# Six graph-attention layers on one core: layer 1's transposed input in another PSUM bank, and another order for the last group's layers

## What is computed

```python
# layer 0: 8 heads of width 32, biases, output projection
q, k, v = x @ Wq + bq, x @ Wk + bk, x @ Wv + bv
x = norm(x + concat_heads(softmax(mask(q k^T / sqrt(32))) v) @ Wo + bo)
# layer 1: one head of width 256, no projection biases
x = norm(x + softmax(mask((x Wq)(x Wk)^T / 16)) (x Wv) Wo + bo)
# layers 2 to 5: q and k of width 128 with biases, values are x itself, then Wc
x = norm(x + softmax(mask(q k^T / sqrt(128))) x Wc^T)
```

## Time and profile before

| | us |
|---|---|
| median of 3 runs | 2370.72 |
| lowest and highest run | 2369.71, 2372.63 |
| profiled execution, its own time | 2373.87 |
| span of its instructions | 2372.1 |
| TensorE busy in it | 2259.9 (95%) |
| DVE, ACT, POOL busy | 1783.3 (75%), 1620.0 (68%), 1794.9 (76%) |
| mean granted TensorE clock | 0.99 |

### The profile page before, as it was taken

One profiled execution on the slowest core, in us unless ns is written; L12 is line 12 of the kernel. 1 busy time (PEld: TensorE's weight loads), 2 busy tenths in 40 slices (PEclk: granted clock), 3 DMA queues, 4 the chain that ended last, 5 costly groups with the idle time before them and its releaser, 6 DMA issues.

```text
span 2372.1 us, 59576 instructions
## 1 busy us (share of the span) xinstructions
PE 2259.9 (95%) x20624; PEld 2136.2 (90%) x20624; DVE 1783.3 (75%) x7734; ACT 1620.0 (68%) x5515; POOL 1794.9 (76%) x2399
## 2 busy tenths in 40 slices
PE   6899999999999999999999999999999999999985
PEld 5799999999999999999999999999999999999974
DVE  4777777777877877877877877877777777777864
ACT  5667767767767767767767767766766766767742
POOL 3368878878878878878878878878878878878751
PEclk9999999999999999999999999999999999999998
DMA  4000000100110000010010000000010010000000
GB/s 154 20 23 24 30 28 24 30 28 25 29 28 25 29 28 26 28 28 26 28 28 27 27 28 28 26 28 28 26 28 28 26 28 28 26 29 17 15 10 14
DMA packets 38747, 68.78 MB, mean 29 GB/s; under 512 B 4400, under 2 KB 12848, under 8 KB 37936
## 3 DMA queue, kind: packets, MB, share of 16 engines
q1 hardware_dynamic: 38448, 64.97, 9.0%
HBM read 48.18 MB, written 16.78 MB: 27 GB/s over the span
## 4 chain that ended last, share of the span: by engine, by line
PE 80%; DVE 9%; ACT 7%; issue 2%; POOL 1%; DMA 0%; POOLq 0%; SPq 0%; DVEq 0%
PE value_bank L450 17%; PE qk_bank L442 16%; PE context_bank L595 9%; PE unit_bank L450 7%; PE unit_bank L442 7%; PE qk_bank L549 7%; PE score_bank L579 5%; ACT probs L676 5%; PE unit_bank L506 4%; PE unit_bank L518 3%; DVE scores L820 2%; PE score_bank L576 2%; PE score_bank L586 2%; DVE xT_lo L854 2%; DVE scores L860 1%
## 5 line engine op out<-in xcount | busy, mean ns | idle before, releaser
L1046 POOL TENSOR_TENSOR x<-y,rows 128x512 f32<-128x512 f32 x305 | 392.0, 1285 | 188.9 <-DVE y L913 188.9
L698 ACT CAST xT_hi<-qk_bank 128x512 fp32r<-128x512 f32 x320 | 187.7, 587 | 399.8 <-PE qk_bank L549 399.6
L676 ACT ACTIVATE probs<-scores,negmax 128x128 f32<-128x128 f32 x1024 | 399.1, 393 | 88.6 <-DVE negmax L820 88.6
L913 DVE TENSOR_SCALAR y<-y,mv,rstd 128x256 f32<-128x256 f32 x730 | 304.2, 459 | 191.6 <-POOL rstd L1030 191.3
L442 PE MATMUL qk_bank<-xT_hi,w_lo 128*128 128x256 f32 x1280 | 411.5, 321 | 21.6 <-DVE xT_lo L854 21.3
L1054 POOL TENSOR_TENSOR x<-x,rows 128x512 f32<-128x512 f32 x305 | 393.8, 1291 | 19.2
L450 PE MATMUL value_bank<-w_lo,xT_hi 128*128 128x256 f32 x1280 | 394.4, 308 | 0.0
L442 PE MATMUL qk_bank<-xT_lo,w_hi 128*128 128x256 f32 x1280 | 363.5, 284 | 0.0
L442 PE MATMUL qk_bank<-xT_hi,w_hi 128*128 128x256 f32 x1280 | 362.1, 283 | 0.0
L450 PE MATMUL value_bank<-w_hi,xT_lo 128*128 128x256 f32 x1280 | 361.8, 283 | 0.0
L450 PE MATMUL value_bank<-w_hi,xT_hi 128*128 128x256 f32 x1280 | 361.0, 282 | 0.0
(11 more groups left out here) (93 smaller groups left out, 6503.3 us busy)
## 6 DMA issues: line engine op xcount, KB each, us to landing
x0T<-xT_in SPq DMA_DIRECT2D x64, 256.0 KB, 3.0
x<-x_in SPq DMA_DIRECT2D x64, 256.0 KB, 3.0
out<-x_out SPq DMA_DIRECT2D x64, 256.0 KB, 2.3
adj<-adj_in SPq DMA_DIRECT2D x64, 128.0 KB, 2.2
late_weights<-w_in SPq DMA_DIRECT2D x2, 1024.0 KB, 7.1
rows<-rows_in SPq DMA_DIRECT2D x1, 1792.0 KB, 11.7
probs0T<-w_in SPq DMA_DIRECT2D x4, 256.0 KB, 4.2
x<-w_in SPq DMA_DIRECT2D x1, 1024.0 KB, 13.2
```

What stands on the lines that cost most here:

```text
L676: e = act.activation(probs0[:, j, g, quad], scores0[:, j, g, quad], ACT.Exp, scale=-1.0, bias=negmax0[:, j, g, quad:quad + 1], accum_out=t ...
L913: m = dve.tensor_scalar(y[:, r, g], y[:, r, g], mv[:, r, g, 0:1], rstd[:, r, g:g + 1], ALU.subtract, ALU.mult)
L1046: pool.tensor_tensor(result(norm), y[:, NORM_AT[norm] % YS], row_of_each(f"gamma{layer}"), ALU.mult).then_inc(zg_ready, 1)
```

## The change

1. For layer 1 of groups 1 to 63, the transposed input goes to `unit_bank[0]`, a bank of layer 0, instead of `qk_bank`. TensorE's transposition waits for the next group's first row maximum (which has read that bank) instead of for ACT's move out of `qk_bank`; that second wait moves to `project_qk`. The next group's transposed probabilities of unit 0 wait for the `xT` copy.
2. The plain copy `xT` moves out of `split_hi` to a place behind the softmax of the item before (`move_xT`), and `split_lo` no longer waits for it.
3. The layers of group 63 stand three slots apart: 315, 318, 321, 324, 327. The items behind slot 315 are 316 5/60, 317 4/61, 318 2/63, 319 3/62, 320 5/61, 321 3/63, 322 4/62, 324 4/63, 325 5/62, 327 5/63. Scores are made early from slot 318, the late half of the values is dropped there, and slot 315's norm takes the DVE-only form.
4. The loops of TensorE, ACT and DVE stop after slot 320. The last seven items p to e (3/62, 5/61, 3/63, 4/62, 4/63, 5/62, 5/63) follow in orders written out by hand. SP and POOL keep their loops.

```diff
-MOVED = {LAST_FIRST + 11: LAST_FIRST + 13}
+MOVED = {LAST_FIRST + 4: LAST_FIRST + 3, LAST_FIRST + 3: LAST_FIRST + 4, LAST_FIRST + 6: LAST_FIRST + 5,
+         LAST_FIRST + 8: LAST_FIRST + 6, LAST_FIRST + 12: LAST_FIRST + 9, LAST_FIRST + 11: LAST_FIRST + 10,
+         LAST_FIRST + 16: LAST_FIRST + 12}
+LAST_ITEMS = [LAST_FIRST + n for n in (4, 5, 6, 7, 9, 10, 12)]
+LOOP_SLOTS = range(FIRST, LAST_ITEMS[2])
...
-    return not item(i + 1) or i > LAST_FIRST + STEP
+    return not item(i + 1) or i >= LAST_FIRST + 3
...
+    return norm[1] < STEP * (LAYERS - 3) or norm[1] >= LAST_FIRST
...
-    return i % PERIOD == STEP
+    return i % PERIOD == STEP and i < LAST_FIRST
...
+        def xT_bank(i):
+            return unit_bank[0] if item(i)[0] == 1 and NTH[i] > 0 else qk_bank
...  # transpose_probs0
+                if j == 0 and group > 1:
+                    pe.wait_ge(xT_ready, group)
...  # transpose_x
-                if NTH[i] > 0:
+                psum = xT_bank(i)
+                if psum is not qk_bank:
+                    pe.wait_ge(negmax0_ready, after_unit(min(group + 1, GROUPS - 1), 0))
+                elif NTH[i] > 0:
                     pe.wait_ge(qk_ready, NTH[i])
...  # project_qk
+                if xT_bank(i) is not qk_bank:
+                    pe.wait_ge(qk_ready, NTH[i])
+                elif layer == 1:
+                    pe.wait_ge(xT_ready, group + 1)
...  # TensorE, after the loop
+            p, q, a, b, c, d, e = LAST_ITEMS
+            context(p); project_qk(a); transpose_probs(q); project_v(a, 0); score(a)
+            context(q); project_v(a, 1); transpose_x(b); transpose_probs(a); context(a)
+            project_qk(b); project_v(b, 0); score(b); project_v(b, 1); transpose_x(c)
+            transpose_probs(b); project_qk(c); context(b); project_v(c, 0); score(c)
+            project_v(c, 1); transpose_probs(c); context(c); transpose_x(d); project_qk(d)
+            project_v(d, 0); transpose_x(e); score(d); project_v(d, 1); project_qk(e)
+            transpose_probs(d); project_v(e, 0); score(e); context(d); project_v(e, 1)
+            transpose_probs(e); context(e)
...  # ACT
-                if layer == 1:
-                    act.copy(flat3(xT[:, :]), qk_bank[:, :]).then_inc(xT_ready, 1)
+            def move_xT(i):
+                act.wait_ge(xT_lo_ready, after(i))
+                act.copy(flat3(xT[:, :]), xT_bank(i)[:, :]).then_inc(xT_ready, 1)
...
                 if item(i - 1):
                     softmax(i - 1)
+                if item(i) and item(i)[0] == 1:
+                    move_xT(i)
...  # ACT, after the loop
+            split_hi(a); move_v(q); softmax(q); move_qk(a); move_probsT(q); softmax(a); move_v(a)
+            split_hi(b); move_probsT(a); move_qk(b); softmax(b); split_hi(c); move_probsT(b)
+            move_v(b); move_qk(c); softmax(c); move_v(c); move_probsT(c); split_hi(d); move_qk(d)
+            split_hi(e); move_v(d); softmax(d); move_qk(e); move_probsT(d); softmax(e); move_v(e)
+            move_probsT(e)
...  # DVE: split_lo, and normalise_alone cut in two
-                if layer == 1:
-                    dve.wait_ge(xT_ready, group + 1)
-                else:
-                    dve.wait_ge(xT_hi_ready, after(i))
+                dve.wait_ge(xT_hi_ready, after(i))
+            def normalise_alone(norm):
+                finish(norm, centre(norm))
...  # DVE, after the loop
+            row_max(q); split_lo(a); add_residual(p); statistics(p); reciprocal_total(q)
+            normalise_alone(p); row_max(a); add_residual(q); statistics(q); reciprocal_total(a)
+            split_lo(b); add_residual(a); statistics(a); centred = centre(a); row_max(b)
+            finish(a, centred); split_lo(c); normalise_alone(q); reciprocal_total(b)
+            add_residual(b); row_max(c); statistics(b); reciprocal_total(c); normalise_alone(b)
+            add_residual(c); statistics(c); split_lo(d); normalise_alone(c); split_lo(e)
+            row_max(d); reciprocal_total(d); add_residual(d); row_max(e); statistics(d)
+            reciprocal_total(e); normalise_alone(d); add_residual(e); statistics(e)
+            normalise_alone(e)
```

More of the change, by code:

```diff
@@ L61 @@
 LAST_FIRST = PERIOD * (GROUPS - 1)
-MOVED = {LAST_FIRST + 11: LAST_FIRST + 13}
+MOVED = {LAST_FIRST + 4: LAST_FIRST + 3, LAST_FIRST + 3: LAST_FIRST + 4, LAST_FIRST + 6: LAST_FIRST + 5,
+         LAST_FIRST + 8: LAST_FIRST + 6, LAST_FIRST + 12: LAST_FIRST + 9, LAST_FIRST + 11: LAST_FIRST + 10,
+         LAST_FIRST + 16: LAST_FIRST + 12}
+PLACED = {slot: regular for regular, slot in MOVED.items()}
+LAST_ITEMS = [LAST_FIRST + n for n in (4, 5, 6, 7, 9, 10, 12)]
+LOOP_SLOTS = range(FIRST, LAST_ITEMS[2])
 def item(i):
-    if i in MOVED:
+    if i in MOVED and i not in PLACED:
         return None
-    for start, moved in MOVED.items():
-        i = start if i == moved else i
+    i = PLACED.get(i, i)
     layer = 1 if i % PERIOD == 0 else LAYERS - i % PERIOD
@@ L117 @@
 SCALED_AT = {n: at for at, n in enumerate(n for n in NORMS if not alone(n))}
-ALONE_AT = {n: at for at, n in enumerate(n for n in NORMS if alone(n))}
+ALONE = [n for n in NORMS if alone(n)]
+_q, _a = ALONE.index(("item", LAST_ITEMS[1])), ALONE.index(("item", LAST_ITEMS[2]))
+ALONE[_q], ALONE[_a] = ALONE[_a], ALONE[_q]
+ALONE_AT = {n: at for at, n in enumerate(ALONE)}
 def layer_and_group(norm):
@@ L643, in _ @@
                     fuse_layer1()
+            p, q, a, b, c, d, e = LAST_ITEMS
+            context(p)
+            project_qk(a)
+            transpose_probs(q)
+            project_v(a, 0)
+            score(a)
+            context(q)
+            project_v(a, 1)
+            transpose_x(b)
+            transpose_probs(a)
+            context(a)
+            project_qk(b)
+            project_v(b, 0)
+            score(b)
+            project_v(b, 1)
+            transpose_x(c)
+            transpose_probs(b)
+            project_qk(c)
+            context(b)
+            project_v(c, 0)
+            score(c)
+            project_v(c, 1)
+            transpose_probs(c)
+            context(c)
+            transpose_x(d)
+            project_qk(d)
+            project_v(d, 0)
+            transpose_x(e)
+            score(d)
+            project_v(d, 1)
+            project_qk(e)
+            transpose_probs(d)
+            project_v(e, 0)
+            score(e)
+            context(d)
+            project_v(e, 1)
+            transpose_probs(e)
+            context(e)
         @block.scalar
@@ L784, in _ @@
                     split_later(LATER_SLOTS.index(i + LATER_LEAD))
+            p, q, a, b, c, d, e = LAST_ITEMS
+            split_hi(a)
+            move_v(q)
+            softmax(q)
+            move_qk(a)
+            move_probsT(q)
+            softmax(a)
+            move_v(a)
+            split_hi(b)
+            move_probsT(a)
+            move_qk(b)
+            softmax(b)
+            split_hi(c)
+            move_probsT(b)
+            move_v(b)
+            move_qk(c)
+            softmax(c)
+            move_v(c)
+            move_probsT(c)
+            split_hi(d)
+            move_qk(d)
+            split_hi(e)
+            move_v(d)
+            softmax(d)
+            move_qk(e)
+            move_probsT(d)
+            softmax(e)
+            move_v(e)
+            move_probsT(e)
         @block.vector
@@ L921, in finish_or_normalise, with centre, finish @@
                     normalise(norm)
-            def normalise_alone(norm):
+            def centre(norm):
+                layer, group = layer_and_group(norm)
+                at = NORM_AT[norm]
+                r = at % YS
+                dve.wait_ge(stats_ready, at + 1)
+                for g in range(G):
+                    last = note(dve.scalar_tensor_tensor(y[:, r, g], y[:, r, g], mv[:, r, g, 0:1],
+                                                         rows[:, ROWS.index(f"gamma{layer}")], ALU.subtract, ALU.mult))
+                return last
+            def finish(norm, centred):
                 layer, group = layer_and_group(norm)
@@ L930, in normalise_alone @@
                     dve.wait_ge(stored[group % STORES], 16 * (group // STORES))
-                dve.wait_ge(stats_ready, at + 1)
-                for g in range(G):
-                    last = note(dve.scalar_tensor_tensor(y[:, r, g], y[:, r, g], mv[:, r, g, 0:1],
-                                                         rows[:, ROWS.index(f"gamma{layer}")], ALU.subtract, ALU.mult))
                 dve.wait_ge(rstd_ready, at + 1)
                 for g in range(G):
-                    dve.wait_ge(dve_step, last - (G - 1) + g)
+                    dve.wait_ge(dve_step, centred - (G - 1) + g)
                     m = dve.scalar_tensor_tensor(result(norm)[:, g], y[:, r, g], rstd[:, r, g:g + 1],
```

57 lines of the change are left out of this document (48 added, 9 removed).

## The result

The changed kernel takes 2338.29 us in the median of 4 runs (2337.01 to 2338.92), the kernel before 2371.68 in the same comparison. The ratio is 0.9859, with a 95% interval of 0.9842 to 0.9876. That is 33.4 us less; 27 were forecast (2344, range 2326 to 2361).

What follows compares the result with a forecast made beforehand. TensorE's own work was taken as 80% of the chain, its longest steady wait being layer 1's transposition behind ACT's move of k. 11 us (steady part) plus 15.6 (end) gave 27 off 2370.7: 2344 us, range 2326 to 2361.

Steps and rivals of the forecast that it cites:

- The steady part: Layer 1's transposition in the other bank, 62 periods: about 0.18 us saved per period, 11 us in all.
- The end: Last group's layers in the new order: 17.1 us less, minus 1.5 for the clock, gives 15.6 us.
- Its own input: Layer 1's transposition next waits for POOL's x, ending 1204.83; TensorE starts 0.58 us earlier, not the whole stall.
- The score product behind the copy of the probabilities: Layer 1's scores wait for ACT's copy of the transposed probabilities; of the 0.58 us, 0.21 are left.
- The row maximum behind DVE's normalisation: DVE first finishes another item's normalisation, waiting for POOL's rstd; row maxima still end at 1207.10, the 0.21 us gone.
- xT_lo no longer waits for the copy: "what remains is the order of the copies": DVE's xT_lo starts right behind the row maxima, 0.15 to 0.23 us earlier; the projection starts 0.22 earlier.
- ACT's 0.53 behind the softmax, price 0.05: The moved plain copy shifts ACT's work up to the next xT_hi by about 0.53 us; DVE gets it 0.05 late.
- the 0.22: Layer 1's projection starts at 1207.77 instead of 1207.99, the gain per period before 0.05 us is taken off.
- To slot 318, and three slots: Slot 318's transposition comes at 2289.1, 0.88 us late; slots 318 to 320 take 6.3 each, so a comes at 2308.0.
- a, c, e in the hand order: Last group's layers 3, 4, 5: 14.2 us from a to c, 14.8 to e, 15.1 to the last norm's end.
- The rivals: All of the stall back 2292 us (0.07); only end 2355 (0.14); only steady part 2360 (0.08); neither 2370 (0.06); slower 2388 (0.07).
- The slower one, the copy in ACT's dense stretch: ACT's extra 0.53 us reaches TensorE in slot 1 every period, costing 33 against the end's 15.6: 2388 us, chance 0.07.

Runs made afterwards that it cites:

- e1: The kernel before with only the other bank, the moved plain copy and their waits, old end kept: 2355.31 us, ratio 0.9929 to before.
- e7: The changed kernel with half of the next group's first exponentials moved behind ACT's copy of the probabilities in slot 4: 2336.01 us, ratio 0.9857 to before.
- e10: The changed kernel plus e3 and e7, with DVE's normalisation at the end of slot 4 put behind layer 1's row maximum and xT_lo: 2359.85 us.
- e3: The changed kernel with the plain copy back right behind xT_hi, the new bank kept: 2336.46 us, ratio 0.9848 to before.
- e8: The changed kernel with 25 added matmuls, results unused, in three waits of TensorE in the last 35 us: 2338.52 us, ratio 0.9871 to before.
- e9: The changed kernel with the plain copy made twice at its new place, once into an unread tile: 2394.43 us, ratio 1.0104 to before.

## Why the prediction was right, and where it was not

The direction, the two parts and their places were right. The steady part was sized at 11 us and is 17.5 (e1), and the cause that the prediction gave for it was wrong (the copy's place, below). The end was sized at 15.6 and is 15.5 to 15.7.

*Its own input.* Right to 0.02: TensorE starts 0.06 behind POOL's x, 0.60 sooner in the period.

*The score product behind the copy of the probabilities.* Right: 0.20 of wait at 56 of 56 places, and 0.22 left of the 0.60, where 0.21 was forecast.

*The row maximum behind DVE's normalisation.* Right in what holds it now (e7), wrong in its place. The prediction said that the row maxima "still end" where they had. They ended 0.12 sooner. I had counted the normalisation's end as a wall, but DVE's next instruction can start about 0.09 before the last one ends, as its rows in the changed kernel show. Before, the row maximum had started 0.02 behind the normalisation's end and 0.65 behind the start of the score product; now it starts 0.09 before that end, though 0.76 behind the product's start. So before it was the product that held it, and not the normalisation (in e10, with the normalisation out of the way, it starts 0.65 behind the product's start too). The projection therefore came 0.34 sooner and not 0.22.

*xT_lo no longer waits for the copy: "what remains is the order of the copies".* This step failed as a cause. The plain copy's new place was worth nothing (e3). The prediction held the old copy at its old time, 1207.21, though the transposition in front of it, and so xT_hi and the copy, moves 0.6 sooner with the bank. The wait would have vanished by itself.

*ACT's 0.53 behind the softmax, price 0.05.* The shift was 0.37, as the copy's old place had delayed the softmax too. In this period nothing of it reached TensorE: DVE took slot 1's xT_hi up 0.13 behind its end. The 0.07 lost of the 0.34 went elsewhere, at the projection itself: its second matmul starts 0.29 behind the first instead of 0.23, and the twelve come a little slower. Why was not settled. At slot 1 the gain is 0.27. 62 times 0.27 is 16.7; the prediction's 0.18 gave 11. So the mis-sized term is the 0.22, by 0.09 to 0.12. The rest, up to a mean of 0.32, lies in slots 2 and 3: periods of the kernel before came as 35.60 (most) and 35.47, those of the changed one as 35.20 with few of 35.35. What makes the two kinds is open.

*To slot 318, and three slots.* Forecast 18.1 and 37.0 behind the transposition for slot 315, measured 18.12 (2268.91) and 37.07 (2287.86).

*a, c, e in the hand order.* c was forecast at 51.2 and came at 51.32, e at 66.0 and came at 66.90, the last norm's end at 81.1 and came at 82.79. 1.9 of that is the clock, which was charged apart at 1.5 for one fall: 1.1 at d's projection and 0.75 at e's context product (e8). Without the falls, in e8, c to e takes 14.46 where 14.8 was forecast, and e to the end 15.14 where 15.1 was. The second agreement is partly luck. The last norm took 4.21, not 3.83, since in it too var_eps took 0.51 (2331.21, beside DVE's gamma step from 2331.16); the steps in front of it were 0.3 shorter than forecast.

What the prediction did not say is how much of the old end was the clock. In the kernel before, three projections behind slot 315 took 2.92 to 2.93 instead of 1.69, about 3.7 us together; the new end loses 1.9 to the clock. My estimate from these two is that about 1.8 of the 15.5 come from fewer falls of the clock.

*The rivals.* None came about. The slower one, the copy in ACT's dense stretch, was priced at 0.53 a period if it came through. e9 shows that the next 0.45 on ACT would have cost 0.93, through DVE's queue. So ACT's slack was there, but of the 0.73 that the prediction read only 0.13 were left, since the gain in front uses it up as well, and its price was nearly twice as high. With that 0.45 more on ACT the change is slower than the kernel before (1.0104).

## What to carry to other kernels

When a stall is taken out, move everything behind it to its new time before looking for the next binding wait: a wait that seems to need its own fix may vanish with the first one (here the copy's place, which was changed for nothing). Then follow each engine, not only the freed one, to the first instruction that does not move; a slack is what remains after the gain has been drawn from it. The last few items of a pipeline are a chain, and a sum of hand-offs from one unhindered item, with the queue's order added step by step, predicted it to 2% here, with errors of 0.3 to 0.4 us in single steps.

## What was not expected of the hardware

Two DVE instructions of the normalisation took 0.74, 1.24 or 2.00 us, by what POOL was doing meanwhile. A schedule in which both engines are three quarters busy has such a price in it, and a shift of 0.45 us changed it by 0.76. And the granted clock at the end fell at different places in executions of the same kernel: at d's projection in one, at c's in the other, with 85.6 us for the end both times, and each time again at the last context product.
